# Two small-head attentions on one core: another spread of the maximum pairs, one output projection a unit, one normalising instruction

## What is computed

```python
def _L0_xattn_ref(q, k, v, wq, bq, wk, bk, wv, bv, wo, bo):
    D_MODEL, NUM_HEADS, DEPTH = 256, 16, 16
    qh = _split_heads(q @ wq.T + bq, b)
    kh = _split_heads(k @ wk.T + bk, b)
    vh = _split_heads(v @ wv.T + bv, b)
    logits = jnp.einsum('bhqd,bhkd->bhqk', qh, kh) / jnp.sqrt(16.)
    weights = jax.nn.softmax(logits, axis=-1)
    out = jnp.einsum('bhqk,bhkd->bhqd', weights, vh)
    return out.transpose(0, 2, 1, 3).reshape(b, -1, D_MODEL) @ wo.T + bo
...
x = x + _L0_xattn_ref(_layernorm(x), ctx_1024, ctx_1024, ...)   # "ca": 1024 keys
x = x + _L0_ffn_ref(_layernorm(x), ...)
x = x + _L1_attn_ref(_layernorm(x), ...)                        # "aa": 512 keys, the same form
```

## Time and profile before

| | us |
|---|---|
| median of three runs (5452.29 to 5461.72) | 5458.92 |
| the profiled execution's own time | 5457.07 |
| its span, first to last instruction | 5455.3 |

### The profile page before, as it was taken

One profiled execution on the slowest core, in us unless ns is written; L12 is line 12 of the kernel. 1 busy time (PEld: TensorE's weight loads), 2 busy tenths in 40 slices (PEclk: granted clock), 3 DMA queues, 4 the chain that ended last, 5 costly groups with the idle time before them and its releaser, 6 DMA issues. The chain is left out here.

```text
span 5455.3 us, 70215 instructions
## 1 busy us (share of the span) xinstructions
PE 4904.9 (90%) x23500; PEld 2633.5 (48%) x23500; DVE 3735.7 (68%) x6968; ACT 2826.4 (52%) x6097; POOL 2455.1 (45%) x1424
## 2 busy tenths in 40 slices
PE   5699998589999888798869999999999999999956
PEld 4455555334444365444445555555555555555423
DVE  6666666578888576588756666666666666666588
ACT  3477775167777533366634454445444544454423
POOL 3455554300000011100027777777777777777700
PEclk8799999789999889899979999999999999999977
DMA  4467777633433101744373333333333433343200
GB/s 142 153 243 243 251 245 242 191 74 67 76 66 74 26 0 38 248 80 80 60 228 81 93 93 87 84 93 93 83 88 89 97 83 88 89 97 83 50 35 20
DMA packets 342966, 593.54 MB, mean 109 GB/s; under 512 B 38576, under 2 KB 131824, under 8 KB 341600
## 3 DMA queue, kind: packets, MB, share of 16 engines
q1 hardware_dynamic: 340448, 585.06, 40.1%
q10 hardware_dynamic: 2176, 4.19, 0.2%
HBM read 333.70 MB, written 221.25 MB: 102 GB/s over the span
## 5 line engine op out<-in xcount | busy, mean ns | idle before, releaser
L2425 POOL TENSOR_TENSOR la_acc<-la_acc,la_pr 128x1024 f32<-128x1024 f32 x704 | 1695.6, 2409 | 493.6 <-ACT la_pr L2383 458.2
L2383 ACT ACTIVATE la_pr<-la_s_ps 128x512 f32<-128x512 f32 x1536 | 794.2, 603 | 971.7 <-PE la_s_ps L2235 969.6
L2242 PE MATMUL la_o_ps<-la_pr,la_vf 128*64 128x512 f32 x3072 | 743.8, 605 | 0.0
L2234 PE MATMUL la_s_ps<-la_q_hl,la_k_hh 128*128 128x512 f32 x1536 | 691.9, 450 | 1.7 <-ACT la_q_hs L2359 1.3
L1641 DVE TENSOR_REDUCE ca_mx<-ca_m_ps 128x2 f32<-128x1024 f32 x512 | 600.8, 1217 | 127.0 <-PE ca_m_ps L1501 126.8
L1604 ACT ACTIVATE ca_pr<-ca_s_ps 128x512 f32<-128x512 f32 x1024 | 539.3, 601 | 265.1 <-PE ca_s_ps L1508 262.6
L2452 DVE TENSOR_REDUCE la_mx<-la_m_ps 128x2 f32<-128x1024 f32 x384 | 463.1, 1206 | 213.9 <-PE la_m_ps L2217 206.1
L2235 PE MATMUL la_s_ps<-la_q_hs,la_k_l 65*128 65x512 f32 x1536 | 607.8, 396 | 0.0
L2452 DVE TENSOR_REDUCE la_mx<-la_misc 128x2 f32<-128x1024 f32 x384 | 466.4, 1215 | 0.0
L107 POOL TENSOR_TENSOR ff_ln_var_eps<-ff_ln_mv,g_eps 128x4 f32<-128x4 f32 x32 | 6.7, 208 | 965.3 <-DVE ff_ln_mv L92 965.3
L2234 PEld LDWEIGHTS la_s_ps<-la_q_hl,la_k_hh 128*128 128x128 f32 x1536 | 290.0, 189 | 242.6 <-ACT la_pr L2383 103.4
(11 more groups left out here) (359 smaller groups left out, 8338.9 us busy)
## 6 DMA issues: line engine op xcount, KB each, us to landing
la_k_hh<-scratch_k_high SPq DMA_DIRECT2D x128, 512.0 KB, 6.6
scratch_k_high<-sc_k_high SPq DMA_DIRECT2D x128, 256.0 KB, 2.6
scratch_k_low<-sc_k_low SPq DMA_DIRECT2D x128, 256.0 KB, 2.8
la_w_parts<-scratch_w_parts SPq DMA_DIRECT2D x64, 512.0 KB, 6.3
la_k_l<-scratch_k_low SPq DMA_DIRECT2D x64, 512.0 KB, 8.5
la_vf<-scratch_xv SPq DMA_DIRECT2D x64, 512.0 KB, 4.2
ca_ks<-scratch_k_rows SPq DMA_DIRECT2D x128, 192.0 KB, 6.3
scratch_vaug<-sc_v SPq DMA_DIRECT2D x16, 1024.0 KB, 4.4
```

The source lines that it names most:

```text
L2234: pe.matmul(s_ps[:, bank, :], k_hh[:, par, h, keys], q_hl[:, par, h, :], start=True, stop=False)
L2242: last = pe.matmul(o_ps[XD * h:XD * h + XD, :], vf[:, par, st, XD * h:XD * h + XD], pr[:, st % LAG, h, :], start=(st == 0), stop=(st == XT ...
L2383: act.activation(pr[:, st % LAG, h, :], s_ps[:, (2 * st + h) % 3, :], ACT.Exp, scale=scale).then_inc(p_done, 1)
L2425: pool.tensor_tensor(total, total, exps, ALU.add).then_inc(acc_done, 1)
```

## The change

1. Pairs of a step. Before, each step has two. Now the steps have PAIRS of them: (1, 2, 1, 2, 3, 2, 3, 2) in ca and (1, 3, 1, 3) in aa. `pairs_of` splits them into three places: early (behind score 1), late (behind score 2), behind (after `weigh`). In the steps of projection and turn (kt 0 and 2) the one pair is late. In other steps the first is early, the second late, the third behind.
2. AHEAD is 8 in ca (6 before), and stays 6 in aa.
3. Projections: OUT = 0. From unit 5 on each unit has one, in its step 0, for 128 tokens of the batch before. `on_t` has two buffers, by the batch's parity, and ACT's wait before it writes `on_t` is one batch looser. Behind the last unit five projections are left, where there were four.
4. `normalise` multiplies all four blocks of 128 queries in one instruction instead of four.

```diff
-    AHEAD = 6
-    TURN, BACK, OUT = 2, 3, ((1, 0), (1, 1), (1, 3), (2, 0))
+    AHEAD = {8: 8, 4: 6}[KT]
+    OUT, TURN, BACK = 0, 2, 3
+    PAIRS = {8: (1, 2, 1, 2, 3, 2, 3, 2), 4: (1, 3, 1, 3)}[KT]
...
-        if unit > GROUPS and (unit % GROUPS, kt) in OUT:
-            yield "project", NT * (unit // GROUPS - 1) + OUT.index((unit % GROUPS, kt))
+        if kt == OUT and unit > GROUPS:
+            yield "project", unit - GROUPS - 1
...
-        first = MP * (unit + 1) + AHEAD + 2 * kt
-        return [j for j in (first, first + 1) if j < MP * UNITS]
+        first = MP * (unit + 1) + AHEAD + sum(PAIRS[:kt])
+        pairs = [j for j in range(first, first + PAIRS[kt]) if j < MP * UNITS]
+        if kt in (OUT, TURN):
+            return [], pairs, []
+        return pairs[0:1], pairs[1:2], pairs[2:]
...
-        on_t = pool_.sb("on_t", [P, KD, T])
+        on_t = pool_.sb("on_t", [P, 2, KD, T])
...
                         scores(unit, u, kt, 2)
-                        if not late:
-                            for j in pairs[1:2]:
-                                max_pair(j)
+                        for j in late:
+                            max_pair(j)
                         scores(unit, u, kt, 3)
...
-                        if late:
-                            for j in pairs[1:2]:
-                                max_pair(j)
+                        for j in behind:
+                            max_pair(j)
...
-                    for qt in range(NT):
-                        last = dve.tensor_tensor(on[:, qt, 64 * (unit % 2):64 * (unit % 2) + 64].rearrange("p (h d) -> p h d", h=GH),
-                                                 heads[:, qt, :, 0:DH], inv[:, qt, :].unsqueeze(2).broadcast_to([P, GH, DH]),
-                                                 ALU.mult)
-                    last.then_inc(on_done, 1)
+                    dve.tensor_tensor(on[:, :, half].rearrange("p q (h d) -> p q h d", h=GH), heads[:, :, :, 0:DH],
+                                      inv[:, :, :].unsqueeze(3).broadcast_to([P, NT, GH, DH]), ALU.mult).then_inc(on_done, 1)
```

More of the change, by code:

```diff
@@ L1353, in attention @@
     S_BANKS = 3
-    AHEAD = 6
-    TURN, BACK, OUT = 2, 3, ((1, 0), (1, 1), (1, 3), (2, 0))
+    AHEAD = {8: 8, 4: 6}[KT]
+    OUT, TURN, BACK = 0, 2, 3
+    PAIRS = {8: (1, 2, 1, 2, 3, 2, 3, 2), 4: (1, 3, 1, 3)}[KT]
+    assert sum(PAIRS) == MP
     scale = DH ** -0.5
@@ L1380, in attention @@
         for kt in range(KT):
-            pairs = pairs_of(unit, kt)
+            early, late, behind = pairs_of(unit, kt)
             for h in range(GH):
@@ L1384, in attention @@
                 if h == 1:
-                    for j in pairs[0:1]:
+                    for j in early:
                         m_turns.add("max", j)
@@ L1388, in attention @@
                         (s_turns if kind == "back" else m_turns).add(kind, n)
-                if h == 2:
-                    for j in pairs[1:2]:
-                        m_turns.add("max", j)
+            for j in late + behind:
+                m_turns.add("max", j)
     m_turns.add("turn", UNITS - 1)
     s_turns.add("back", UNITS // 2 - 1)
-    for j in range(NT):
-        m_turns.add("project", NT * (B - 1) + j)
+    for n in range(UNITS - GROUPS - 1, UNITS):
+        m_turns.add("project", n)
     with ExitStack() as ctx:
@@ L1539, in project @@
                     for k in range(KD):
-                        last = pe.matmul(out[:, 0, 0:D], on_t[:, k, j * P:(j + 1) * P], w_o[:, k, :], start=(k == 0), stop=(k == KD - 1))
+                        last = pe.matmul(out[:, 0, 0:D], on_t[:, b % 2, k, j * P:(j + 1) * P], w_o[:, k, :],
+                                         start=(k == 0), stop=(k == KD - 1))
                     last.then_inc(proj_ready, 1)
@@ L1555, in _ @@
                     for kt in range(KT):
-                        pairs = pairs_of(unit, kt)
+                        early, late, behind = pairs_of(unit, kt)
                         scores(unit, u, kt, 0)
                         scores(unit, u, kt, 1)
-                        for j in pairs[0:1]:
+                        for j in early:
                             max_pair(j)
-                        late = False
                         for kind, n in after(unit, kt):
@@ L1584, in _ @@
                 turn_back(UNITS // 2 - 1)
-                for j in range(NT):
-                    project(NT * (B - 1) + j)
+                for n in range(UNITS - GROUPS - 1, UNITS):
+                    project(n)
             @block.scalar
@@ L1597, in keep_back @@
                     act.wait_ge(back, pair + 1)
-                    act.wait_ge(proj_ready, NT * (pair // KD))
-                    act.activation(on_t[:, pair % KD, :], s_ps[:, s_turns.bank("back", pair), :], ACT.Copy).then_inc(on_t_done, 1)
+                    if pair >= 2 * KD:
+                        act.wait_ge(proj_ready, NT * (pair // KD - 1))
+                    act.activation(on_t[:, pair // KD % 2, pair % KD, :], s_ps[:, s_turns.bank("back", pair), :], ACT.Copy).then_inc(on_t_done, 1)
                 def weight(unit, kt, h):
@@ L1660, in normalise @@
                     dve.wait_ge(back, unit // 2)
-                    for qt in range(NT):
-                        last = dve.tensor_tensor(on[:, qt, 64 * (unit % 2):64 * (unit % 2) + 64].rearrange("p (h d) -> p h d", h=GH),
-                                                 heads[:, qt, :, 0:DH], inv[:, qt, :].unsqueeze(2).broadcast_to([P, GH, DH]),
-                                                 ALU.mult)
-                    last.then_inc(on_done, 1)
+                    half = slice(64 * (unit % 2), 64 * (unit % 2) + 64)
+                    dve.tensor_tensor(on[:, :, half].rearrange("p q (h d) -> p q h d", h=GH), heads[:, :, :, 0:DH],
+                                      inv[:, :, :].unsqueeze(3).broadcast_to([P, NT, GH, DH]), ALU.mult).then_inc(on_done, 1)
                 def add_output(n):
@@ L1689, in _ @@
                                 add_output(n)
-                        for j in pairs[1:2]:
+                        for j in late + behind:
                             reduce_pair(j)
                 normalise(UNITS - 1)
-                for j in range(NT):
-                    add_output(NT * (B - 1) + j)
+                for n in range(UNITS - GROUPS - 1, UNITS):
+                    add_output(n)
 FFN_BLOCKS = 3
```

2 lines of the change are left out of this document (removed).

## The result

| | median us | runs | against the runs of before beside them |
|---|---|---|---|
| before | 5458.01 | 18 (5445.4 to 5464.6) | |
| changed | 5465.72 | 18 (5453.2 to 5476.3) | 1.0016, 95% interval 1.0008 to 1.0023 |

The change makes the kernel slower by 0.16%, 9 us (4 to 13). The forecast was 36 us over: the direction and the stage that loses are right, the size is four times too large. 5465.72 lies under the 5475 to 5512 of "my case". The profiled execution has a span of 5458.2 us. In what follows all ratios are of fast runs; one of aa_alone's twelve runs was slow (6096.5 us at a granted clock of 0.73), and stands in its median but not in its ratio.

A forecast was written before the change was run, and what follows sets the result against it. A loop of PE and ACT was taken as the bound, not DVE. Ca +32.7 (pairs +72.6, turn and back -14.1, projections -25.8) and aa +4.4 made +37 on the profiled 5457: 5494 us, range 5450 to 5512.

The forecast's parts named there:

- my case: The whole kernel: main forecast of 5494 us, within 5475 to 5512, chance 0.70.
- steps 4 to 7, third pairs: Ca: third pairs behind weigh and the waits in the steps after them, +2.42 us a unit, +72.6 in all.
- projection: Ca step 0: projection and one late pair take 3.43 us, +0.77 over a plain step.
- turn: Ca step 2: turn and one late pair take 2.95 us, +0.29 over a plain step.
- back, half a unit's: Ca step 3 in each second unit: four transposes between two pairs, +0.62 us, so 0.31 a unit.
- g: Ca steps 0, 2 and 3: score 2 to late pair where nothing holds it back, taken as 0.24 us.
- aa: Stage aa: +4.4 us; units 5 to 29 gain 6.5, units 1 to 4 lose 6.6, the ends lose 2.4 + 0.5 + 1.4.
- the fifth closing projection: End of each stage: one more projection behind the last unit, about 1.4 us.
- the clock: Main forecast: steady at 1.00. Rival: falls for two steps of each unit, 56 us more, 5550, chance 0.05.
- the second rival: No measurable change: half the waits absorbed, about 5460 us, chance 0.13; or low-end steps and negate hidden, 5475.
- negate in the way of the third reduction: Ca step 4: negate takes 0.60 us, so the third reduction starts at 3.63 where its matmuls would allow 3.33.
- the first rival: Faster: the wait behind the third pair does not come in ca and aa, 63 us less, about 5430, chance 0.12.

The follow-up runs named there:

- aa_alone: The changed attention in aa, the attention of before in ca; 5444.03 us, 0.9964 of before.
- triples_moved: The changed kernel with ca's three-pair steps at 1 and 7 instead of 4 and 6; 5435.14 us, 0.9959 of before.
- two_everywhere: The changed kernel with two pairs in each step of both stages and no third pair; 5418.89 us, 0.9934 of before.
- normalise_alone: The kernel before with only the single normalising instruction put in; 5452.99 us, 0.9994 of before.
- ahead6: The changed kernel with AHEAD = 6 in ca instead of 8; 5453.31 us, 0.9998 of before.
- triples_moved_ahead7: As triples_moved, with AHEAD = 7 in both stages; 5427.04 us, 0.9937 of before.
- two_late: As triples_moved_ahead7, with step 1's third pair put back into step 0, both late there, and AHEAD 7 and 6; 5398.77 us, 0.9901 of before.

## Why the forecast was right in its sign and wrong in its size

The mechanism stands. A third pair behind weigh costs its own 0.46 and makes PE wait in the next step if that has two pairs; moved (triples_moved) the wait goes, taken away (two_everywhere) the change becomes a gain. By terms, ca first, in us a unit:

| term | forecast | the trace after | what it makes in us |
|---|---|---|---|
| steps 4 to 7, third pairs | +2.42 | +2.37 (3.99 + 2.67 + 3.72, less 3 x 2.67) | forecast 72.6, is 71 |
| projection | +0.77 | +0.60 | 20.8, is 16.2 |
| turn | +0.29 | +0.14 | with the back: |
| back, half a unit's | +0.31 | +0.24 | 18.6, is 11.8 |
| granted clock | 0 | | 0, is 6.7 in this trace |

**One step that failed is g**, the distance from score 2 to the late pair. The trace of before bounded it by 0.10 and 0.34 and I took 0.24, the middle. It is 0.01, under both bounds. Not all of the 0.23 came back, since a neighbour was longer each time: scores to projection or turn are 0.42 to 0.44 and not 0.34, and in the step of the back late pair to weigh is 0.90 and not 0.80. So the three terms that had this g were too high by 0.17, 0.15 and 0.12, and 11 us in all. Where two bounds come from rows, the row that is closest in form should win over the middle: the plain step's 0.10 is the same pair behind the same score.

**The larger one is aa**, +4.4 in the forecast and -11.5 in the traces; 1.4 of the forecast are the fifth closing projection, which stands behind the last weigh, so between the weighs +3.0 stands against -11.5, a miss of 14.5. Its steady unit was right within 0.14 (13.42 against 13.28, waits 4.00 and 3.73 from weigh to weigh against 3.95 and 3.72), which is 3.5 us. The edges were wrong:

- For units 1 to 4 I let step 0's late pair wait for the third pair of step 3 as in the units with a projection. But the two halves of the PSUM are handed out in rotation, and without a projection in between the pair takes the half of the *second* pair of step 3, long free: 3.02 instead of 3.74 from weigh to weigh. These units lose 1.7 us and not 6.6.
- The same holds for unit 0's missing turn (2.66 in step 2 to 3). Unit 0 was to lose 2.4 us and gains 0.4.
- Unit 29 has the last of the old clusters. It takes 13.01 us instead of 16.03, 3.0 less, where the forecast had a mean gain of 0.26.

Together 10.4 us.

**The third is the clock**, put at nothing: its falls behind the wait of step 5 cost 6.7 us in ca in this trace. And the fifth closing projection, priced at 1.4 us in each stage, costs nothing, as its rows under normalise_alone show.

The balance: 34 of the forecast's 37 us lie between first and last weigh. Less 13 for ca's terms and 14.5 for aa, and 7 more for the clock, that is 14; ca's ends take off 3 (unit 31 took 21.6 us before, mostly at the low clock, and 19.2 now), which gives the 10.5 of the traces. The medians say 9 (4 to 13). This lies near the 5460 of the second rival, and inside the 11 us to which I gave 0.13, but not by its mechanism: the waits behind the third pairs were not absorbed, they have the size forecast.

Right as forecast: negate in the way of the third reduction (it starts straight behind negate; taken out of the three-pair step it is 0.12 a unit in ahead6, and moved to where DVE is idle 0.21 in triples_moved_ahead7, where the sum had 0.30), normalisation and second `on_t` buffer at nothing (normalise_alone for the first; the second was not tried alone), the first rival's waits not going away.

Of the rivals the clock was half true. I gave 0.05 to two steps in every unit; it is one to two steps in four to nine units of 32. I had read from the 0.94 us waits of the kernel before, at a steady 1.00, that 0.8 us waits are harmless. In this order they are not: the clock fell behind waits of 0.82, and of 0.66 in ahead6. So the length of a single wait does not tell the two apart. The Trainium skill, "TensorE: Matmul & The Clock Gate", section "A second HAM failure mode: psum-queue depth-cycling", describes short idle times between groups that cycle through PSUM banks as a reason for the clock to swing; in the middle of ca the trace of before does not agree, and the traces with third pairs in steps 4 and 6 show falls as it describes them (0.71 in 1320 to 1330 us), though no run here shows that the idle times are their cause.

What stays open: why the clock falls behind some of these waits and not behind others, what decides the clock at ca's ends, and how much of it is in the medians.

## What to carry to other kernels

With two buffers between a producer and a slower consumer, look at the spacing of the uses and not at their number in a step: a use put off to the end of one step makes the second use of the next step wait for the consumer. Here that was 0.57 to 0.82 us of waiting ahead of a second pair and 0.45 behind the short turn; ahead of a step whose first use is long (the projection) the wait went, and only the pair's own 0.46 was left. Trace the hand-out order of the buffers for each kind of step on its own, the first and last units too. And the best place for an extra use was beside the long operation that the consumer clears fast: a second pair behind the projection cost 0.48 us in two_late and 0.59 in two_everywhere, against 0.46 + 0.60 behind weigh.

## What the hardware showed that I had not expected

After a projection or a turn in ca, a maximum pair starts 0.01 us behind the score ahead of it, and score 3 follows 0.46 us later. The granted clock fell from 1.00 to 0.50 behind a wait of 0.82 us (0.66 in ahead6) in some units and not in others of the same form, at places that differ between two executions of the same program: four units in one, nine in the other, and ca 8 us longer. The kernel before, with waits of 0.94 us, kept 1.00.
